# The TensorE stream of an attention-and-FFN kernel: a loop over pairs of ticks against ticks written out

## The reference

```python
k = rope((x @ Wk.T), 16 heads of 32);  v = x @ Wv.T
for chunk of 16 tokens:                      # a scan over 256 chunks, state W per batch and head, 32x32
    z = k_c @ W
    W = W - k_c.T @ ((z - v_c) * 2/(16*32))
out = layernorm(z) * gamma + beta;  x1 = layernorm(x + out @ Wo.T)
g = (x1 @ gate_w.T) * gate_s;  u = (x1 @ up_w.T) * up_s         # 1408 wide
return layernorm(x1 + ((silu(g) * u) @ down_w.T) * down_s)
```

## Time and profile before

| what | value |
|---|---|
| median of three runs | 2095.89 us |
| the profiled execution's own time | 2094.25 us |
| its span, first to last instruction | 2092.5 us |
| TensorE matmuls (PE) busy | 1966.8 us, 94% of the span |
| VectorE / ScalarE / GpSimd busy | 58% / 45% / 28% |
| mean granted TensorE clock | 0.967 |

### The profile page before, as it was taken

One profiled execution on the slowest core, in us unless ns is written; L12 is line 12 of the kernel. 1 busy time (PEld: TensorE's weight loads), 2 busy tenths in 40 slices (PEclk: granted clock), 3 DMA queues, 4 the chain that ended last, 5 costly groups with the idle time before them and its releaser, 6 DMA issues.

```text
span 2092.5 us, 59019 instructions
## 1 busy us (share of the span) xinstructions
PE 1966.8 (94%) x22424; PEld 1565.2 (75%) x22424; DVE 1218.8 (58%) x2814; ACT 938.9 (45%) x2258; POOL 581.9 (28%) x651
## 2 busy tenths in 40 slices
PE   5669999999999999999999999999999999998987
PEld 4347777778877777787777788777777877777775
DVE  3475565656656565655656565565666556665532
ACT  2334444444444444444444444444444444444421
POOL 2002332323332232323223232322223322322222
PEclk9669999999999999999999999999999999999998
DMA  6742322222332222232222223221222322222110
GB/s 213 254 134 73 91 85 78 65 75 73 92 90 85 68 72 77 72 92 87 85 66 77 74 77 92 83 87 55 75 77 88 92 82 82 64 84 55 47 36 21
DMA packets 210992, 176.58 MB, mean 84 GB/s; under 512 B 34192, under 2 KB 165520, under 8 KB 210576
## 3 DMA queue, kind: packets, MB, share of 16 engines
q1 hardware_dynamic: 210768, 173.08, 27.6%
HBM read 105.86 MB, written 75.76 MB: 87 GB/s over the span
## 4 chain that ended last, share of the span: by engine, by line
PE 89%; DVE 5%; issue 2%; ACT 2%; SPq 1%; DMA 1%; POOL 0%; POOLq 0%; DVEq 0%
PE gu_acc L623 35%; PE work L604 27%; PE down_acc L635 14%; PE state_acc L594 4%; PE z_acc L577 4%; PE work L611 3%; PE gu_acc L611 1%; DVE err L806 1%; DVE fm L835 1%; ACT fm L482 1%; SPq L293 1%; DVE hid L813 1%; DVE low_half L871 1%; ACT hid L458 1%; DMA v_rows<-v_scr 0%
## 5 line engine op out<-in xcount | busy, mean ns | idle before, releaser
L806 DVE TENSOR_TENSOR err<-z_acc,v_rows 32x256 f32<-32x256 f32 x1024 | 430.2, 420 | 197.4 <-PE z_acc L577 168.3
L385 POOL TENSOR_TENSOR hid_lo<-hid,hid_hi 128x256 fp32r<-128x256 f32 x352 | 266.4, 757 | 954.0 <-ACT hid_hi L468 953.8
L434 ACT ACTIVATE state<-state_acc 32x256 f32<-32x256 f32 x1028 | 384.7, 374 | 89.7 <-PE state_acc L594 65.2
L623 PE MATMUL gu_acc<-x_hi,gw 128*128 128x256 f32 x1408 | 390.2, 309 | 8.7 <-DVE x_lo L850 3.6
L623 PE MATMUL gu_acc<-x_hi,uw 128*128 128x256 f32 x1408 | 355.5, 284 | 0.0
L623 PE MATMUL gu_acc<-x_lo,uw 128*128 128x256 f32 x1408 | 354.9, 284 | 0.0
L623 PE MATMUL gu_acc<-x_lo,gw 128*128 128x256 f32 x1408 | 354.2, 284 | 0.0
L813 DVE SCALAR_TENSOR_TENSOR hid<-gu_acc,up_scale,hid 128x256 f32<-128x256 f32 x352 | 170.1, 483 | 316.0 <-ACT hid L458 315.1
L447 ACT ACTIVATE v_rows<-z_acc 128x256 f32<-128x256 f32 x256 | 98.4, 384 | 542.3 <-DVE err L806 542.3
L623 PEld LDWEIGHTS gu_acc<-x_hi,gw 128*128 128x128 f32 x1408 | 269.1, 191 | 60.6 <-issue 24.5
L635 PE MATMUL down_acc<-dw,hid_hi 128*128 128x512 f32 x704 | 286.2, 407 | 2.8 <-POOL hid_lo L385 2.8
(11 more groups left out here) (67 smaller groups left out, 2185.4 us busy)
## 6 DMA issues: line engine op xcount, KB each, us to landing
x_fm<-xT SPq DMA_DIRECT2D x64, 256.0 KB, 3.1
k_scr<-k_tok SPq DMA_DIRECT2D x32, 512.0 KB, 3.1
k_rows<-k_scr SPq DMA_DIRECT2D x512, 32.0 KB, 1.8
v_rows<-v_scr SPq DMA_DIRECT2D x512, 32.0 KB, 1.8
z_scr<-v_rows SPq DMA_DIRECT2D x512, 32.0 KB, 1.6
z_tok<-z_scr SPq DMA_DIRECT2D x32, 512.0 KB, 4.1
x_tok<-x SPq DMA_DIRECT2D x32, 512.0 KB, 3.7
out<-x_tok SPq DMA_DIRECT2D x32, 512.0 KB, 2.9
```

Source lines behind the costliest of these rows:

```text
L385: pool.tensor_tensor(hid_lo[m % RING][:], hid[m % 2][:], hid_hi[m % RING][:].bitcast(F32), ALU.subtract).then_inc(hid_lo_ready, 1)
L434: act.activation(state[q, :, e].rearrange("p (r g) e -> p r g e", r=2), state_acc[q, :, 0:P].rearrange("p r (g e) -> p r g e", e=HEAD), AC ...
L623: mm = pe.matmul(gu_acc[:, k * TOK:(k + 1) * TOK], lhsT=w[:, c, m * P:(m + 1) * P].bitcast(dt), rhs=part[:, c].bitcast(dt), start=(c == 0 ...
L806: dve.tensor_tensor(err[q, g:g + 2, :, :].rearrange("p a (r h) e -> p a r (h e)", r=2), z_acc[q, :, 0:P].rearrange("p r (a c) -> p a r c", ...
```

## The change

TensorE's two calls of `run` become calls of a new helper without a loop. Both arms of the branch now hold ticks 3 to 35 written out, with constants in every wait. The work, its order and its waits within a tick are the same. The other four engines still call `run` and keep their loop over pairs.

```diff
@@ -232,6 +232,10 @@
             for t in range(LAST, NT + 4):
                 tick(Nth(t))
 
+        def run_straight(tick, begin):
+            for t in range(begin, NT + 4):
+                tick(Nth(t))
+
         def rows(n, b=None, first=0, count=P):
 
@@ -743,9 +747,9 @@
             with pe.If(inexact == 0):
-                run(pe, lambda t: tick(t, F32R), 3)
+                run_straight(lambda t: tick(t, F32R), 3)
             with pe.Else():
-                run(pe, lambda t: tick(t, F32), 3)
+                run_straight(lambda t: tick(t, F32), 3)
```

## The result

The changed kernel took 2058.67 us as the median of four runs (2056.58 to 2059.67), the kernel before 2094.31 us in its four; the ratio is 0.9829, with a 95% interval of 0.9811 to 0.9847. The forecast was 2059 us. The profiled execution took 2059.66 us with a span of 2057.8 us.

What follows compares the result with a forecast made beforehand. TensorE's matmuls, busy 94% of the span, were taken to bound the kernel. Idle time of 22.8 us plus 12.8 us, mostly clock, gave 35.6 us off 2094.25, so 2058.6, put down as 2059 us; range 2053 to 2066.

Steps and rivals of the forecast that it cites:

- The idle time at the turn: TensorE idle before the tick-opening `z_acc` at 12 loop turns; straight code removes all of it, 22.8 us.
- The slow clock: TensorE's clock falls behind turns; without the pause it stays at 1.00 throughout, 12.8 us taken from the sum.
- The check in the prediction: Cross-check of the slow clock's size: eight falls of 1.36 us make 10.9 us, about the same as 12.8.
- Constants in the waits, at nothing: Constants take register instructions off TensorE's stream; worth 0.01 us a tick at most, priced at nothing.
- The even tick's 0.08 us: Even looped ticks stay at 59.92 us against 59.83, through ScalarE's `copy_v`, because ScalarE keeps its loop.
- Straight code at nothing: Reading TensorE's 26 written-out ticks in order costs nothing; the high bound was 296 us.
- The other engines' turns: The other engines' loop turns lose the cover of TensorE's pause; taken as nothing, VectorE's at most 1.1 us a turn.
- The sum: Ticks 4 to 29 go from 1592.46 to 1556.88 us, a gain of 35.6 us.
- The rivals: Clock still falls, 2071.4 us, 0.05; another engine's turn, 0.04; straight code starved, 0.02; jump not the cause, 2094 us, 0.03.
- the starved stream: Rival: late instruction blocks stop TensorE in straight code; gain gone at 0.23 us a block, 2137 us at 0.5; chance 0.02.

Runs made afterwards that it cites:

- near jump: The changed kernel with a jump over 8 never executed matmuls at each of the 12 places where the loop turned; 2058.13 us.
- long pause made with GpSimd: The changed kernel, with TensorE waiting for three GpSimd additions at the 12 places of the old turns; 2094.07 us.
- hinted loop: The kernel before, with TensorE's loop option that names the coming jump at the head of each iteration; 2058.39 us.
- far jumps: The changed kernel with 12 jumps over 1300 never executed matmuls each, 2104.85 us; with all targets placed close to their block's end, 2139.99 us.
- loop cut at slot 4: The kernel before, with TensorE's loop iterations beginning at slot 4 of an even tick instead of slot 0; 2069.67 us.
- short GpSimd pause: The changed kernel, with TensorE waiting for one GpSimd addition at the 12 places of the old turns; 2068.14 us.
- loop over fours: The kernel before, with TensorE looping over four ticks instead of two, 5 turns instead of 12; 2071.46 us.

## Why the prediction was right

*The idle time at the turn* was priced at 22.8 us and went completely. That it is the reading of the jump's target is shown from four sides: a near jump costs nothing, a far one without a loop costs the same, a hinted turn costs nothing, and the place of the target in its block of 256 instructions decides whether a second pause follows.

*The slow clock* was most of the other 12.8 us, which came from the sum, as what was left. In the stretch after, the clock never falls below 1.00. The check in the prediction, eight times 1.36 us, took the smallest of the eight falls: pairs of ticks behind a fall took 1.35 to 1.54 us more than pairs without one, about 11.9 us in all. The rest is mostly in the odd ticks, 59.90 us up to the last matmul before and 59.83 after. That the fall follows the pause and not the jump is shown by the long pause made with GpSimd.

*Constants in the waits, at nothing:* the hinted loop, which keeps its registers, takes 1556.72 us for the 26 ticks, the written-out one 1556.74.

*The even tick's 0.08 us:* it stayed with TensorE written out (59.91 and 59.92 us) and went with ScalarE written out.

*Straight code at nothing:* no pause in 1556.74 us. The instruction queue carries 134 blocks of 16 KB in the last 24 ticks of the stretch, 5.6 a tick, against 155 before:

```profile
q8 instruction: 134, 2.20, 0.7%
```

*The other engines' turns:* for VectorE the bounds were 0 to 2.46 us a turn; ScalarE and SyncE had no bound in the rows. VectorE's first `err` behind its own turn now stands idle 0.50 us, released by `z_acc`, where it was 2.46 us in the earlier trace rows; nothing of TensorE's idle time hid a turn of VectorE. And the only wait of PE left in the stretch is the one of 0.2 us a tick, so no other engine's turn held it either.

```profile
344.34 1.77 DVE L810 TENSOR_TENSOR err<-z_acc,v_rows 32x256 f32<-32x256 f32 x4 [0.50 <-PE z_acc L581]
```

*The sum:* 35.7 us measured against 35.6 in the looped stretch. That the total agrees to 0.3 us is partly luck: 2059 was chosen between 2058.6, reckoned from the profiled execution, and 2060.3, reckoned from the median, and 2.3 us were lost before tick 4 and 1.3 us gained behind tick 29, which the prediction had left in its range.

*The rivals:* none occurred. The clock didn't fall in the stretch, no engine's turn took the place, and the idle times went. The nearest to a real danger is the starved stream: the far jumps show what late blocks do, 2139.99 us with 24 pauses. Straight code read in order had no such pause in 134 blocks; how near it comes to one wasn't measured.

## What to carry to other kernels

Where the engine that bounds the kernel stands idle for "issue" at the turn of a loop and nowhere else, price the idle time and look at the clock behind it, since here a pause of 1.9 us cost on average another 1.1 us, mostly in slow matmuls. Writing out the stream, naming the jump ahead with a hint, and putting the turn where much work is queued all help (35.7, 35.7 and 24 us here); the hint keeps the code small. Read the cost of each from ticks without a turn in the same trace: they are the kernel after the change.

## What the runs showed of the hardware that was not expected

A far jump can cost twice. With the target 37 to 59 instructions ahead of the end of its block of 256, a second pause of 2.3 to 3.1 us followed each jump, and the kernel took 56 us more than with the target 197 to 219 instructions ahead (2139.99 against 2083.96 us).

Pauses of 0.65 to 1.15 us, twelve in a kernel, left the clock at 1.00 (the loop cut at slot 4, and the short GpSimd pause); pauses of 1.7 to 2.3 us brought it to 1.2 GHz behind some turns and not behind others, one of five in the loop over fours and eight of twelve in the kernel before. Behind twelve pauses of 1.84 us each, made with GpSimd, it fell eight times and stayed four times, so the length of the pause alone doesn't decide. What does is open.
